# Two residual tiles for each stream, the next input asked for at the head of a turn, and the table request of the second experts moved into their inner loop

## The chip, the cores and the metric

The kernel runs on one NeuronCore of one Trainium2 chip, in one launch. The metric is the device time of the launch in microseconds (us); of several runs the median is given. TensorE does matmuls, VectorE and ScalarE element-wise work, GpSimd the small powers, memsets and indexed transfers, and SyncE (SP) starts transfers (DMA) between HBM and the on-chip memory. In the profile these engines are PE (PEld for its weight loads), DVE, ACT, POOL and SP. Each engine runs its own list of instructions in order; they meet in semaphores.

## What is computed

A decoder of four layers over 32 sequences of 128 tokens with 128 features. Each layer has three sections, and each section adds its result to the residual x after a layer norm:

```python
x = x + L0_attn(layernorm(x))           # delta rule with convolutions and a gate over four paths
x = x + L0_xattn(layernorm(x), ctx)     # 16 heads
x = x + L0_ffn(layernorm(x))
x = x + L1_attn(layernorm(x))           # 16 heads, causal
x = x + L1_xattn(layernorm(x), ctx)     # a mix with the mean of the context
x = x + L1_ffn(layernorm(x))            # 8 experts, 2 chosen, and a shared one
x = x + L2_attn(layernorm(x))           # 16 heads, causal, rotary
x = x + L2_xattn(layernorm(x), ctx, mask)
x = x + L2_ffn(layernorm(x))            # 14 experts, 1 chosen, GELU
x = x + L3_attn(layernorm(x))           # state-space scan
x = x + L3_xattn(layernorm(x), ctx, key_padding)
x = x + L3_ffn(layernorm(x))            # 8 experts, 1 chosen, limited capacity
```

The "second experts" are L2_ffn: for each of 14 experts `gelu(x @ w1 + b1) @ w2 + b2`, weighted and summed. L3_ffn depends on the order of all tokens, so the main loop only scatters each token's row to its expert's place in HBM, and a final stage computes those experts.

## The kernel before

**Streams and rounds.** Two streams work at once on every engine, each on a group of 2 sequences (256 tokens): stream 0 begins a round with L0_delta, stream 1 with L1_mix (ROUND, TURN and FIRST near the top of the file). A round has all twelve sections for both. Stream 0 therefore hands over from one group to the next at the end of a round, stream 1 in the middle of it, between L3_moe and L0_delta. There are 8 groups for each stream. They are run as a first stretch (stream 1 alone, L0_delta to L1_attn), a loop with a body of two rounds that runs three times, and a last stretch of one round and one part named "last". In the body the rounds are turn 0 and turn 1. A stretch and each pass of the loop body end with a barrier of all engines, before which SP waits until the awaited inputs have landed (`landed`, lines 2510 to 2513) and after which it clears the semaphores.

**The order.** Each section gives, for each engine, a Python generator, and the order of the two streams' steps on an engine is written out by hand as strings (TURNS and END_TURNS): "0" and "1" take the next step of that stream. On TensorE a "w" stands for one filler matmul of the identity (`warm`, line 2548), which keeps the engine active and whose result nobody reads. The order never depends on what is ready: an engine stands at its next instruction until its semaphores allow it. PSUM is a ring of 8 banks; an engine waits for a full bank with `P.take` and frees it with `P.give`.

**The residual.** Each stream has one tile `xres` of 128 x 2 x 128 floats. `norm_dve` (lines 694 to 708) reads it, `residual_dve` (line 714) and the second experts (line 1387) add to it, and in L3_moe line 1437 copies it into the rows to be scattered. SP's part of a handover is `stored` and `load`: it waits until the rows are made (`e3.placed`), starts the store of `xres` to the output (line 2455), waits for it and for the two indexed transfers of GpSimd (line 2459), and then starts four transfers, one for the next `xres` (line 2439) and three for the context, the mask and the key padding (lines 2440 to 2442). VectorE waits for the first of them (semaphore `s_in`) ahead of L0_delta's norm. That wait also keeps L0_delta from writing over the rows in the shared scratch before they have been scattered, since SP starts the input only behind them. SP's own order for two rounds is the string "011100011100".

At stream 1's handover, VectorE's order is: the norm of stream 0's cross attention (line 708 for 0_hn), the statistics of stream 1's new input (line 694), then for stream 0 the keys (line 996) and the masked keys (line 1006), whose first half TensorE's scores (line 864) wait for, then stream 1's normalized rows (line 708 for 1_hn) and the maxima of the scores (line 1013). GpSimd's part of L0_delta begins with one power for the norm and, when TensorE's transposes have been copied to hT, three memsets in the scratch (lines 2360 to 2362).

**Activation tables.** ScalarE can evaluate one set of functions at a time; a change of set is one instruction, ACT_TABLE_LOAD. `Tables.use` (line 429) asks for a set unless its record `now` says that it is in place. The record follows the order in which the steps of both streams are written out. In the second experts the request for the GELU set stands at the head of an expert, two steps of the order ahead of its first half:

```python
for e in range(E2):
    yield
    tables.use(act, GELU)
    for c in range(2):
        yield
        t = P.take(act, f"{nm}.u{e}.{c}")
```

Between these yields the other stream's attention may ask for the EXP set (line 977). Where an activation is reached with another set in place than it needs, the compiler puts a table load of its own ahead of it; the profile shows such a load with the line of the activation. For the first half of an expert from the fourth on, ScalarE waits for two banks (the one to read, and that of the expert three before, whose hidden rows it writes over); such a double wait is an instruction of its own.

## Time and profile before

| | us |
|---|---|
| median of 3 runs | 4257.61 |
| lowest and highest | 4251.89, 4261.13 |
| the profiled execution | 4248.77 |
| its span, first to last instruction | 4246.9 |
| TensorE busy | 3921.6 (92%) |
| VectorE busy | 3004.1 (71%) |
| ScalarE busy | 1983.9 (47%) |
| GpSimd busy | 655.7 (15%) |
| mean granted TensorE clock | 0.963 |

The busy times come from one execution recorded by the hardware profiler; the span is its own, and 1.9 us lie around it. A wait is written as "idle, <- who ended it"; "issue" stands where the profile names no releaser. Times "at" a point are microseconds from the start of the span. A row of the timeline can merge instructions of one kind that follow each other (x2, x8). The granted clock is a share of 2.4 GHz: 1.00 is 2.4, 0.50 is 1.2, and a value between is the mean over a stretch that has both.

### The profile page before, as it was taken

What the parts mean: (1) busy time and instruction counts of PE and PEld (TensorE: products, weight loads), DVE (VectorE), ACT (ScalarE), POOL (GpSimd) and SP (SyncE); (2) the same over time, 40 slices, a digit from 0 to 9 for tenths busy, and PEclk for the clock granted to TensorE, in tenths of its full rate; (3) what the DMA queues carried; (4) which work ended last, traced back from release to release, by engine and by line L of the source; (5) the groups of instructions that cost most, each with busy time, mean ns of one, the idle gap of its engine ahead of it and who ended that gap; (6) DMA issues with size and microseconds to landing.
All of it is one profiled execution on the core that took longest, in us unless ns stands there. A gap on an engine that the chain in (4) does not pass through costs nothing. (4 is left out here: it accounts for less than half of the span.)

```text
span 4246.9 us, 103906 instructions
## 1 busy us (share of the span) xinstructions
PE 3921.6 (92%) x42881; PEld 2849.9 (67%) x42881; DVE 3004.1 (71%) x7740; ACT 1983.9 (47%) x4472; POOL 655.7 (15%) x924
## 2 busy tenths in 40 slices
PE   4889999899998999989999899999999899999998
PEld 3667676667766676766866667666676667666685
DVE  5558786586865867768776787758786586876762
ACT  2355443655336453464534644365443655336441
POOL 2200212101120111201111020200212102120003
PEclk7899999999999989999999999999999999999999
DMA  3300000000000000000000000000000000000011
GB/s 92 76 2 1 10 1 10 1 3 8 9 2 1 9 2 9 2 1 9 2 9 2 1 9 2 9 2 1 10 1 10 1 1 9 8 2 1 3 37 66
DMA packets 52824, 46.08 MB, mean 11 GB/s; under 512 B 8354, under 2 KB 48914, under 8 KB 52126
## 3 DMA queue, kind: packets, MB, share of 16 engines
q1 hardware_dynamic: 48076, 32.94, 2.9%
q8 instruction: 346, 5.67, 0.6%
q0 software_dynamic: 2560, 5.79, 0.4%
q14 instruction: 128, 1.05, 0.1%
q10 hardware_dynamic: 1714, 0.63, 0.1%
HBM read 27.25 MB, written 12.62 MB: 9 GB/s over the span
## 5 line engine op out<-in xcount | busy, mean ns | idle before, releaser
L2548 PE MATMUL banks<-ident_bf 128*128 128x256 bf16 x6321 | 1004.5, 279 | 32.1 <-ACT scratch L979 11.5
L2548 PEld LDWEIGHTS banks<-ident_bf 128*128 128x128 bf16 x6321 | 619.0, 101 | 250.8 <-issue 78.7
L1013 DVE TENSOR_REDUCE scratch<-banks 128x4 f32<-128x512 f32 x512 | 321.8, 683 | 64.6 <-PE banks L837 29.7
L979 ACT ACTIVATE scratch<-banks 128x512 f32<-128x512 f32 x512 | 274.0, 598 | 148.8 <-PE banks L834 70.8
L1842 DVE TENSOR_TENSOR_SCAN scratch<-scratch 128x512 f32<-128x512 f32 x256 | 312.6, 1221 | 8.9 <-ACT scratch L1785 3.8
L1021 DVE RECIPROCAL scratch<-banks 128x128 f32<-128x128 f32 x128 | 122.4, 957 | 273.7 <-PE banks L919 247.3
L429 ACT ACT_TABLE_LOAD x242 | 310.5, 1283 | 6.3 <-PE banks L1189 2.0
L864 PE MATMUL banks<-scratch 32*128 32x512 f32 x2048 | 307.2, 654 | 4.7 <-issue 3.9
L1697 PE MATMUL banks<-scratch,w_ident 128*128 128x256 f32 x1024 | 268.3, 384 | 17.1 <-DVE scratch L1848 17.0
L685 POOL TENSOR_TENSOR 0_rstd<-0_var,minus_half 128x2 f32<-128x2 f32 x96 | 68.9, 718 | 1343.5 <-DVE 0_var L703 1030.9
L1785 ACT ACTIVATE scratch<-scratch,ssm_A 128x256 f32<-128x256 f32 x512 | 226.2, 500 | 98.0 <-DVE scratch L1842 91.3
L1362 ACT ACTIVATE scratch<-banks,w_e_b 128x256 f32<-128x256 f32 x448 | 195.0, 472 | 157.3 <-PE banks L1318 153.6
L919 PE MATMUL banks<-scratch 128*32 128x128 f32 x4096 | 216.7, 284 | 53.6 <-ACT scratch L979 52.2
L1326 PE MATMUL banks<-experts,scratch 128*128 128x128 f32 x1792 | 249.2, 286 | 6.5 <-DVE scratch L2249 5.9
L1983 PEld LDWEIGHTS banks<-scratch 32*32 32x32 f32 x10496 | 196.4, 114 | 86.9 <-issue 64.6
L1326 PEld LDWEIGHTS banks<-experts,scratch 128*128 128x128 f32 x1792 | 236.1, 199 | 26.0 <-issue 17.0
L1983 PE MATMUL banks<-scratch 32*32 32x32 f32 x10496 | 232.0, 201 | 15.3 <-issue 12.2
L685 POOL TENSOR_TENSOR 1_rstd<-1_var,minus_half 128x2 f32<-128x2 f32 x96 | 70.3, 732 | 939.5 <-DVE 1_var L703 671.5
L919 PE MATMUL banks<-scratch,w_slots 128*32 128x128 f32 x4096 | 209.9, 277 | 0.0
L1697 PEld LDWEIGHTS banks<-scratch,w_ident 128*128 128x128 f32 x1024 | 178.0, 190 | 47.4 <-DVE scratch L1848 23.8
L1238 ACT ACTIVATE scratch<-banks 128x256 f32<-128x256 f32 (+1 forms) x224 | 84.8, 383 | 251.8 <-PE banks L1189 251.3
L690 ACT COPY 0_hT<-banks 128x256 f32<-128x256 f32 x96 | 35.8, 373 | 349.2 <-PE banks L680 349.2
(515 smaller groups left out, 8041.5 us busy)
## 6 DMA issues: line engine op xcount, KB each, us to landing
expert_in<-scratch SPq DMA_DIRECT2D x1, 4112.0 KB, 27.0
experts<-in_e_W SPq DMA_DIRECT2D x14, 256.0 KB, 5.3
scratch<-expert_in SPq DMA_DIRECT2D x2, 1542.0 KB, 11.2
w_e_W<-in_e_W SPq DMA_DIRECT2D x3, 704.0 KB
experts<-in_e_w SPq DMA_DIRECT2D x1, 1792.0 KB, 8.2
experts<-in_e_w SPq DMA_DIRECT2D x2, 896.0 KB, 12.3
scratch<-expert_in SPq DMA_DIRECT2D x2, 514.0 KB, 4.4
1_xres<-in_x SPq DMA_DIRECT2D x8, 128.0 KB, 2.2
```

The source lines that it names most:

```text
L429: act.preload_act_table_set(name)
L864: last = pe.matmul(row_tiles(t), lhs[r, col(s)], rhs[r, s], start=True, stop=letter == "S" and mask is None, skip_group_check=True)
L919: last = pe.matmul(t[32 * i:32 * i + 32, k * L:(k + 1) * L], W["slots"][:, 32 * j:32 * j + 32] if k else vslot[:, s, j, i, :], pT[:, s % 2 ...
L979: P.give(act.activation(pT[:, s % 2, j, :], t, ACT.Exp), f"{nm}.T{s}{j}")
L1013: P.give(dve.tensor_reduce(negm[:, s, NI * j:NI * j + NI], row_tiles(t), X, ALU.max, negate=True), f"{nm}.S{s}{j}")
L1326: last = pe.matmul(t[:, col(s)], hid[:, e % RING, c, col(s)], w2[:, 2 * e + c, :], start=c == 0, stop=c == 1, skip_group_check=True)
L1362: P.give(act.activation(hid[:, e % RING, c, :], t, ACT.Gelu, bias=W["e2_b1"][:, 2 * e + c:2 * e + c + 1]), f"{nm}.u{e}.{c}")
L1697: last = pe.matmul(total[:, c * N:(c + 1) * N], ident[:], yc[:, k % RING, j, :], start=False, stop=n == DS - 2 and j == 1, skip_group_chec ...
L1785: ins = act.activation(decay[:, k % RING, j, :], dstart[:, c, :], ACT.Exp, scale=ssm_A[:, c, n + j:n + j + 1])
L1842: dve.tensor_tensor_scan(*flat, 0.0, ALU.mult, ALU.add).then_inc(ev(nm + ".state"), 1)
L1983: last = pe.matmul(t[dst, h * width:(h + 1) * width], lhs(h), rhs(h), start=True, stop=True, skip_group_check=True)
L2548: pe.matmul(banks[:, bank, 0:N].rearrange("p (s f) -> p s f", s=G), ident_bf[:], spread(ident_bf[:], G), start=True, stop=True, skip_group ...
```

## The change

It has two parts.

1. In the second experts, `tables.use(act, GELU)` moves from the head of an expert to the head of each of its two halves, behind the yield and ahead of the wait for the bank.
2. Each stream gets two residual tiles, `residual[0]` and `residual[1]`. `xres(name)` picks one by the turn and, for stream 1, by whether the section belongs to the group that the round began with or to the next. The input for the next group is started at the head of a turn (`load_x`), into the tile that is not in use; the context, the mask and the padding are started where they were (`load_ctx`). As VectorE's wait for the input no longer says anything of the scattered rows, SP adds 1 to a new semaphore, `s_taken`, when the store and the scatter are done, and GpSimd waits for it ahead of L0_delta's memsets. The new semaphore is cleared with the others.

```diff
--- before.py
+++ after.py
@@ -390,6 +390,7 @@
         self.ring.wait_given(eng, self.tag + name)
 
 
+KEYS = ["d0", "x0", "f0", "a1", "m1", "e1", "a2", "x2", "e2", "s3", "x3", "e3"]
 PER_PASS = {
     ".ctx.maskf": 1, ".ctx.ms": 1, ".ctx.n": 1, ".ctx.padrow": 1, ".ctx.rms": 1, ".ctx.sq": 1,
     "d0.Nb": 2 * G, "d0.T": 5 * G, "d0.TT": G, "d0.diag": 2 * G, "d0.feat": 1, "d0.inverse": 1, "d0.kb": 2, "d0.mid": 1,
@@ -627,7 +628,7 @@
 
         def stream(u):
             scratch = scratches[u]
-            xres = sb(f"{u}_xres", [128, G, D])
+            residual = [sb(f"{u}_xres{k}", [128, G, D]) for k in range(2)]
             ctx_tok = sb(f"{u}_ctx_tok", [128, G, D])
             ctxT = sb(f"{u}_ctxT", [128, N])
             ctxnT = sb(f"{u}_ctxnT", [128, N])
@@ -645,7 +646,7 @@
             var, rstd, rms, rms2 = (sb(f"{u}_{n}", [128, G]) for n in ("var", "rstd", "rms", "rms2"))
             place = sb(f"{u}_place", [128, G], U32)
             token = W["token"][:, TURN[u] * G:TURN[u] * G + G]
-            s_scatter = sem(f"rows_placed{u}")
+            s_scatter, s_taken = sem(f"rows_placed{u}"), sem(f"rows_taken{u}")
             s_in, s_out, s_ctx = sem(f"group{u}_loaded"), sem(f"group{u}_stored"), sem(f"context{u}_loaded")
             def program(ring, passes):
                 stacks, norms, shared = {}, {}, {}
@@ -655,8 +656,15 @@
                     P = PassBanks(ring, turn)
                     loads = 1 if part == "first" else turn + (ROUND[u][0] != "L0_delta")
 
+                    ended = 0 if part == "first" else loads
+                    lead = len(SECTIONS) - ROUND[u].index("L0_delta") if FIRST[u] and part == "round" else 0
+
                     def before(name):
                         return turn * PER_PASS[name[1:]]
+
+                    def xres(name):
+
+                        return residual[(turn + (KEYS.index(name[1:3]) < lead)) % 2]
 
                     ctx = f"{u}.ctx"
 
@@ -691,7 +699,7 @@
 
                     def norm_dve(dve, q, nm, rms_too=False):
                         for s in range(G):
-                            m = q.mark(dve.bn_stats(stats[:, s, :], xres[:, s, :]))
+                            m = q.mark(dve.bn_stats(stats[:, s, :], xres(nm)[:, s, :]))
                         first = m - G + 1
                         for s in range(G):
                             q.wait(first + s)
@@ -705,14 +713,14 @@
                         yield
                         dve.wait_ge(ev(f"{u}.rstd"), norm(nm) + 1)
                         for s in range(G):
-                            dve.tensor_scalar(hn[:, s, :], xres[:, s, :], mv[:, s, 0:1], rstd[:, s:s + 1],
+                            dve.tensor_scalar(hn[:, s, :], xres(nm)[:, s, :], mv[:, s, 0:1], rstd[:, s:s + 1],
                                               ALU.subtract, ALU.mult).then_inc(ev(f"{u}.hn"), 1)
 
                     def residual_dve(dve, q, name):
 
                         t = P.take(dve, name)
-                        P.give(dve.tensor_tensor(xres[:].rearrange("p s f -> p (s f)"), xres[:].rearrange("p s f -> p (s f)"), t,
-                                                 ALU.add), name)
+                        x = xres(name)[:].rearrange("p s f -> p (s f)")
+                        P.give(dve.tensor_tensor(x, x, t, ALU.add), name)
                         P.wait_given(dve, name)
 
                     def bias_row(pe, t, row, start=True):
@@ -1352,9 +1360,9 @@
                             act.activation(lg, tmp, ACT.Exp).then_inc(ev(f"{u}.exp"), 1)
                             for e in range(E2):
                                 yield
-                                tables.use(act, GELU)
                                 for c in range(2):
                                     yield
+                                    tables.use(act, GELU)
                                     t = P.take(act, f"{nm}.u{e}.{c}")
                                     if e >= RING and c == 0:
                                         P.take(act, f"{nm}.d{e - RING}")
@@ -1384,8 +1392,8 @@
                                 yield
                                 t = P.take(dve, f"{nm}.d{e}")
                                 for s in range(G):
-                                    ins = dve.scalar_tensor_tensor(out=xres[:, s, :], in0=t[:, col(s)],
-                                                                   scalar=gate[:, s, e:e + 1], in1=xres[:, s, :],
+                                    ins = dve.scalar_tensor_tensor(out=xres(nm)[:, s, :], in0=t[:, col(s)],
+                                                                   scalar=gate[:, s, e:e + 1], in1=xres(nm)[:, s, :],
                                                                    op0=ALU.mult, op1=ALU.add)
                                 P.give(ins, f"{nm}.d{e}")
                                 P.wait_given(dve, f"{nm}.d{e}")
@@ -1434,7 +1442,7 @@
                             tables.use(act, EXP)
                             act.wait_ge(ev(f"{u}.diff"), base["diff"] + 1)
                             act.activation(lg, tmp, ACT.Exp).then_inc(ev(f"{u}.exp"), 1)
-                            act.copy(rows[:, :, D:2 * D], xres[:]).then_inc(ev(nm + ".placed"), 1)
+                            act.copy(rows[:, :, D:2 * D], xres(nm)[:]).then_inc(ev(nm + ".placed"), 1)
 
                         def dve_f(dve, q):
                             yield from norm_dve(dve, q, nm)
@@ -2357,6 +2365,8 @@
                             norm_pool(pool, nm)
                             yield
                             P.wait_given(pool, nm + ".hT")
+                            if ended:
+                                pool.wait_ge(s_taken, ended)
                             pool.memset(pads[:, :, :, 0:3], 0.0)
                             pool.memset(TT64_flat, 0.0)
                             pool.memset(vpad[:, :, 0:PAD], 0.0).then_inc(ev(f"{u}.zero"), 1)
@@ -2435,11 +2445,17 @@
                     r_d = out.rearrange("(g u s) t f -> u g t s f", u=STREAMS, s=G)[at_v]
                     p_d = dram["key_pad"].rearrange("(g u a s) t -> u g a (s t)", u=STREAMS, a=1, s=G)[at_v]
 
-                    def load(sp, g):
-                        sp.dma_start(xres[:], x_d[g]).then_inc(s_in, 16)
+                    def load_x(sp, g, k):
+                        sp.dma_start(residual[k][:], x_d[g]).then_inc(s_in, 16)
+
+                    def load_ctx(sp, g):
                         sp.dma_start(ctx_tok[:], c_d[g]).then_inc(s_ctx, 16)
                         sp.dma_start(mask_i[:], m_d[g]).then_inc(s_ctx, 16)
                         sp.dma_start(pad_row_u8[:], p_d[g]).then_inc(s_ctx, 16)
+
+                    def load(sp, g):
+                        load_x(sp, g, 0)
+                        load_ctx(sp, g)
 
                     def stored(sp, g):
 
@@ -2452,14 +2468,17 @@
                             for e in range(E3 - 1):
                                 load_expert3(sp, e, s_e3)
                         sp.wait_ge(ev(f"{u}e3.placed"), G + 3 + before(f"{u}e3.placed"))
-                        sp.dma_start(r_d[g], xres[:]).then_inc(s_out, 16)
+                        sp.dma_start(r_d[g], residual[turn % 2][:]).then_inc(s_out, 16)
                         yield
                         sp.wait_ge(s_out, 16 * (turn + 1))
 
                         sp.wait_ge(s_scatter, g * (16 * G) + 16 * G)
+                        sp.sem_inc(s_taken, 1)
 
                     def steps(engine, *args):
 
+                        if engine == 4 and part == "round":
+                            load_x(args[0], args[1] + turn + 1, (turn + 1) % 2)
                         yield
                         for name in order:
                             if name == "L0_delta" and engine == 2 and loads:
@@ -2494,7 +2513,7 @@
                             if name == "L3_moe" and engine == 4:
                                 yield from stored(args[0], args[1] + turn)
                                 if part == "round":
-                                    load(args[0], args[1] + turn + 1)
+                                    load_ctx(args[0], args[1] + turn + 1)
                                 yield
 
                     context = {0: ctx_pe, 1: ctx_act, 2: ctx_dve, 3: ctx_pool}
@@ -2512,7 +2531,7 @@
                     sp.wait_ge(s_in, 16 * total)
                     sp.wait_ge(s_ctx, 48 * total)
 
-                return ones[0][0], landed, steps, [s_in, s_out, s_ctx]
+                return ones[0][0], landed, steps, [s_in, s_out, s_ctx, s_taken]
 
             return program
```

## Rows read from the trace of the kernel before

**Rows 1.** The page: busy time of TensorE, and the filler matmuls of line 2548.

```profile
PE 3921.6 (92%) x42881; PEld 2849.9 (67%) x42881; DVE 3004.1 (71%) x7740; ACT 1983.9 (47%) x4472; POOL 655.7 (15%) x924
...
L2548 PE MATMUL banks<-ident_bf 128*128 128x256 bf16 x6321 | 1004.5, 279 | 32.1 <-ACT scratch L979 11.5
```

**Rows 2.** Waits of TensorE, 153 to 4160 us: total us, times, longest us.

```profile
PE banks L919 <- ACT scratch L979: 51.6, 28, 3.1
...
PE banks L864 <- issue: 3.5, 7, 1.1
```

**Rows 3.** ScalarE's groups: count, busy us, mean ns, idle us before them.

```profile
L429 ACT ACT_TABLE_LOAD x242 | 310.5, 1283 | 6.3 <-PE banks L1189 2.0
...
L1362 ACT ACT_TABLE_LOAD x31 | 39.8, 1283 | 2.0 <-PE banks L1318 0.2
...
L979 ACT ACT_TABLE_LOAD x29 | 37.2, 1283 | 0.5
```

**Rows 4.** Timeline of ScalarE, 295 to 313 us: start, us, what ran, idle before.

```profile
301.23 1.28 ACT L1362 ACT_TABLE_LOAD   x1
...
310.35 1.28 ACT L1362 ACT_TABLE_LOAD   x1 [0.22 <-PE banks L1318]
```

**Rows 5.** Timeline of all engines, 450 to 465 us: a handover of stream 1.

```profile
455.43 0.60 DVE L708 TENSOR_SCALAR 0_hn<-0_xres,0_mv,0_rstd 128x128 f32<-128x128 f32 x2 [0.84 <-POOL 0_rstd L685]
...
456.54 0.40 SPq L2439 DMA_DIRECT2D 1_xres<-in_x  x1
...
457.42 0.59 PE L850 MATMUL banks<-0_ctxT,w_x_Wk 128*128 128x256 f32 x2
...
458.81 0.49 DVE L694 BATCH_NORM_STATS2 1_stats<-1_xres 128x6 f32<-128x128 f32 x2 [2.77 <-DMA 1_xres<-in_x]
...
459.62 0.48 DVE L996 TENSOR_SCALAR scratch<-banks,w_x_bk 128x256 f32<-128x256 f32 x1
...
460.13 1.29 DVE L1006 TENSOR_TENSOR scratch<-scratch,w_in_four 128x512 f32<-128x512 f32 x2
...
460.92 1.14 PE L864 MATMUL banks<-scratch 32*128 32x512 f32 x8 [1.10 <-issue]
...
462.43 2.48 DVE L1013 TENSOR_REDUCE scratch<-banks 128x4 f32<-128x512 f32 x4 [0.48 <-PE banks L837]
...
463.72 0.12 POOL L2360 MEMSET scratch<- 128x18 f32 x1 [2.31 <-ACT 1_hT L690]
```

**Rows 6.** Stream 1's residual tile, idle time before its instructions: us, times.

```profile
  DMA 1_xres<-in_x: 18.6, 8
```

**Rows 7.** Timeline of VectorE, 0 to 5 us.

```profile
3.46 0.48 DVE L694 BATCH_NORM_STATS2 1_stats<-1_xres 128x6 f32<-128x128 f32 x2 [3.46 <-DMA 1_xres<-in_x]
```

**Rows 8.** Timeline, 3506 to 3513 us: the last handover of stream 1.

```profile
3512.01 1.14 PE L864 MATMUL banks<-scratch 32*128 32x512 f32 x8 [0.18 <-issue]
```

**Rows 9.** Timeline, 644 to 664 us: a handover of stream 0.

```profile
654.39 0.38 SPq L2439 DMA_DIRECT2D 0_xres<-in_x  x1
...
660.38 0.48 DVE L694 BATCH_NORM_STATS2 0_stats<-0_xres 128x6 f32<-128x128 f32 x2
```

**Rows 10.** Waits of SP, 1150 to 1180 us, at the end of a loop body.

```profile
SPq L2574 <- PEq L2574: 1.8, 1, 1.8
```

**Rows 11.** SP's line 2459: duration ns min/median/max, first and last start.

```profile
L2459 SPq EVENT_SEMAPHORE  x8: 17/17/17, 654.2 to 3707.7; - x8
```

**Rows 12.** ScalarE's line 2089, its idle time: us, times.

```profile
  POOL scratch L2362: 0.8, 1
```

**Rows 13.** Rounds of stream 0 without a barrier: length, busy us (x), PEclk, DMA share, GB/s.

```profile
1174.83:1690.41 515.58, 487.19 (x5303) 353.53 (x5304) 372.32 (x963) 246.12 (x556) 77.88 (x110) 0.95 0.02 5
...
sum 2031.15, PE 1916.52 PEld 1391.26 DVE 1487.78 ACT 983.88 POOL 311.98; mean PE 479.13 PEld 347.82 DVE 371.94 ACT 245.97 POOL 78.00
```

**Rows 14.** Two stretches, same columns.

```profile
1025.00:1035.00 10.00, 9.89 (x125) 8.38 (x119) 4.02 (x15) 4.82 (x16) 0.71 (x1) 0.92 0.01 2
1035.00:1047.00 12.00, 12.00 (x46) 9.41 (x45) 6.97 (x20) 4.15 (x10) 0.11 (x1) 0.50 0.00 1
```

## The prediction, made before the changed kernel was run

> **What bounds the kernel now.** The page first. TensorE is busy 3921.6 of 4246.9 us, and 1004.5 us of that are 6321 filler matmuls of line 2548, which stand in its fixed order and compute nothing [rows 1]. So a shorter wait elsewhere can give back at most TensorE's own idle time, 4246.9 - 3921.6 = 325 us, and only where TensorE waits for exactly the thing that the change makes earlier. The second view is therefore TensorE's waits between 153 and 4160 us: the longest entry is 51.6 us in 28 waits for the exponentials of line 979; the waits at line 864, for which the profile names no releaser, are 3.5 us in 7 [rows 2]. Then I read ScalarE's groups for the first half of the change, and one handover of a stream for the second.
>
> **Part 1, the table loads.** Line 429, the explicit request, made 242 loads of 1283 ns. 31 more stand at line 1362 and 29 at line 979: there the record of the table in use was out of date, because the other stream had changed the table between two steps, and the load was put in by itself just ahead of the activation [rows 3]. After the change the record is right, so these 60 become explicit loads. ScalarE's order of work is the same, so their number is the same: each of the 60 really changes the set. I found no explicit load that went unused and would now be saved. What changes is only whether a load starts before or after the wait for the bank. The same rows price this: the 29 loads of line 979 sat idle 0.5 us in all, 17 ns each, so they already start without a wait; nothing is to be had there. The 31 of line 1362 sat idle 2.0 us. The floor is 31 x 17 ns = 0.5 us, so the wait that can be covered is 1.5 us. It lies at some loads only: the one at 310.35 began 0.22 us late, the one at 301.23 not at all [rows 4]. Bounds: a gain of 0 (if TensorE doesn't feel it) to 2.0 us. I take **-1.5 us**, since the exponentials behind such loads are what TensorE waits for [rows 2]. The 60 loads themselves, 60 x 1.283 = 77 us of ScalarE, stay.
>
> **Part 2, the input rows.** Stream 1 hands over in the middle of a round. SP waits for its result to be stored and its rows to be scattered, and issues the next input at 456.54. VectorE, done with stream 0's norm at 455.43 + 0.60 = 456.03, stands until 458.81, 2.77 us, for that input [rows 5]. Over the run this wait is 18.6 us in 8 [rows 6]; one of them, 3.46 us, is the very first load [rows 7] and stays. The seven others are 15.1 us. With two tiles the input is issued in the turn before, hundreds of microseconds ahead, so VectorE's 15.1 us go.
>
> What TensorE gets of it is less. Behind the norm VectorE makes the masked keys (lines 996 and 1006), for which TensorE's line 864 waits. TensorE was ready at 460.92 - 1.10 = 459.82. After the change line 996 starts when its bank is full, at 457.42 + 0.59 = 458.01, not at 459.62. The first half of line 1006 then ends 1.6 us earlier, at about 459.2 instead of 460.8, which is 0.6 us before TensorE needs it [rows 5]. So the whole 1.10 us goes here, and not more. In the last of the seven handovers TensorE's wait is only 0.18 us [rows 8]. All seven are the 3.5 us at line 864 [rows 2]. What is late next: VectorE's line 1013 already waits 0.48 us for TensorE's masks [rows 5], so from there TensorE leads and the other engines move with it. I take **-3.5 us**. Bounds: 0, if the shift is lost further on, and 15.1 us, if every microsecond of VectorE counts.
>
> Stream 0 hands over at the end of a round. Its input was issued at 654.39; with the 458.81 - 456.54 = 2.27 us that stream 1's took, it was there by 656.7, but VectorE comes to it at 660.38 without idle time [rows 9]. Gain 0; the cover is some 3.7 us of the other stream's work, which stays. The same holds where the loop body ends: the context loads still follow the store there and are awaited, and when all have landed SP waits a further 1.8 us for TensorE's queue [rows 10]. Leaving the input out lets the context loads go some 0.4 us earlier, into that 1.8 us. I take 0; were TensorE early by over 1.8 us, up to 0.4 us at each of three barriers would be felt.
>
> **What it adds.** The two input loads at the head of a turn cost SP 0.40 us each [rows 5]. Behind them in its queue is only the wait for stream 1's rows, half a round away. At the second turn stream 0's load stands behind its context loads and stream 1's behind that; each is needed only at that stream's next handover. GpSimd gets 11 waits on the new semaphore (7 of stream 1; of stream 0 only the 4 at second turns). Behind each in its queue are the three memsets of the delta section and then its later products, which ScalarE, VectorE and TensorE take up. The semaphore is raised where the input was issued before, at 456.5, while the memsets start at 463.72, released by the hT copy [rows 5]. If TensorE is 1.1 us early, they start at 462.6, still 6 us behind. A satisfied wait I price by SP's plain semaphore instruction, 17 ns [rows 11]: 11 x 17 = 0.2 us on GpSimd, bounds 0 and 0.2, taken as 0, because only one ScalarE copy of the run waited for those memsets, 0.8 us [rows 12].
>
> **Sum.** -1.5 - 3.5 = -5.0 us. The profiled execution took 4248.8 (span 4246.9), so one like it would take 4243.8. The median of the runs, 4257.6, lies 8.8 above it; the prediction is made for that: 4257.6 - 5.0 = **4252.6 us**, -0.12%. About 0.2%, 8.5 us, is what a measurement of this kernel can tell from no change, so this counts as no change.
>
> **Why runs differ.** The four rounds of stream 0 that hold no barrier have the same instructions. One of them took 515.58 us at 0.95 of TensorE's clock; the four together took 2031.15, so the others averaged 505.2 [rows 13]. The excess is 10.4 us, twice my sum. It isn't a matter of long waits: from 1035 to 1047 us TensorE was granted 0.50, 1.2 GHz, though it was busy 9.89 of the 10 us before and 12.00 of the 12 in it [rows 14]. The Trainium skill, "TensorE: Matmul & The Clock Gate", Part 1, has the throttled state as the default, which activity releases; by that rule shorter waits could only raise the clock, and the slower rival below would have no ground. By that rule a fall at a TensorE so busy should not be there, so it isn't relied on here: I leave the clock out of the sum and keep both signs.
>
> **Rivals.**
> - All of VectorE's wait arrives: 15.1 + 1.5 = 16.6 us, 4241.0. It would be so if VectorE set the pace behind the handover. Against it: the 0.48 us for which it waits on TensorE right there [rows 5]. For it: each set of four maxima behind it takes VectorE 2.48 us [rows 5]. Chance 0.12. The Trainium skill, "DMA: Bandwidth & Descriptors", in its rules table, would have the load's fixed cost overlap once it is issued early and waited for late; taken for the time of the kernel, that is this rival.
> - Nothing arrives: the 3.5 us turn up as another wait before the round ends, and the table loads were covered: 4257.6. Against it: TensorE releases every engine that feeds it there. Chance 0.12.
> - Slower, by the clock: the shift of a microsecond moves the dense stretches, and more rounds go as the long one did. It decides from two more: 2 x 10.4 - 5.0 = +15.8, 4273.4; one alone gives +5.4, 4263.0, still no change. Chance 0.08.
> - The same with the other sign: the long round becomes a short one, -10.4 - 5.0 = -15.4, 4242.2. Chance 0.10.
>
> **How the numbers follow.** My forecast has the remaining 0.58, with its own range 4248 to 4258 (the terms between 0 and what I took, and the runs' spread). The range 4242 to 4263 leaves out the first rival and the slower one, 0.20. Faster by over 0.2% is below 4249.1: 0.12 + 0.10, and 0.02 of the forecast, 0.24. Slower is above 4266.1: 0.07, as 0.01 of the slower rival stops at one round. Within: 0.69.
>
> **What would show it.** Right: no table load at lines 1362 and 979, about 302 at line 429, with about 1.5 us less idle before them all; VectorE's wait for the input left only at the start; TensorE's seven waits at line 864 gone; GpSimd's memsets still released by the hT copies. Wrong: another number of table loads; GpSimd waiting for SP; another TensorE wait near the handover grown by what line 864 lost; a round's length changed by more than 2 us at an equal clock.

## The result, and the profile after

| | before | after |
|---|---|---|
| median of 3 runs, us | 4257.61 | 4223.67 |
| lowest and highest, us | 4251.89, 4261.13 | 4217.96, 4225.45 |
| the profiled execution, us | 4248.77 | 4225.45 |
| its span, us | 4246.9 | 4223.6 |
| mean granted TensorE clock | 0.963 | 0.967 |

The ratio of the runs is 0.9934, with a 95% interval from 0.9912 to 0.9955: faster by 0.66%, 28 us by the ratio and 34 by the medians. The same kernel run again, six times against eleven of the kernel before, gave 0.993, 0.9913 to 0.9946. Forecast were 4252.6, in a range from 4242 to 4263. So the kernel gained some 23 to 29 us more than the 5.0 of the sum.

The page of the kernel after, to be held against [rows 1, 3]:

```profile
PE 3903.9 (92%) x42881; PEld 2838.5 (67%) x42881; DVE 3003.1 (71%) x7740; ACT 1980.7 (47%) x4470; POOL 655.9 (16%) x924
...
L2567 PE MATMUL banks<-ident_bf 128*128 128x256 bf16 x6321 | 995.5, 277 | 32.9 <-ACT scratch L987 10.8
...
L430 ACT ACT_TABLE_LOAD x300 | 384.9, 1283 | 7.3 <-PE banks L1197 2.0
```

TensorE has the same 42881 matmuls and is busy 3921.6 - 3903.9 = 17.7 us less; its 6321 fillers take 9.0 us less (277 ns each, not 279). The same work taking less time is the first sign that the clock had a part. All table loads are now at the explicit request, 300, and none is left at the two activations; their idle time is 7.3 us where the three rows of before had 6.3 + 2.0 + 0.5 = 8.8.

TensorE's waits, 153 to 4160 us, against [rows 2] (total us, times, longest):

```profile
PE banks L927 <- ACT scratch L987: 51.1, 29, 3.1
...
PE banks L872 <- ACT scratch L957: 0.8, 1, 0.8
```

The seven waits at the masks' line, 3.5 us, are gone; the one left there, 0.8 us, is ScalarE's. The handover of stream 1, timeline of all engines, against [rows 5]:

```profile
459.90 0.60 DVE L716 TENSOR_SCALAR 0_hn<-0_xres,0_mv,0_rstd 128x128 f32<-128x128 f32 x2 [0.84 <-POOL 0_rstd L693]
...
460.42 0.48 DVE L702 BATCH_NORM_STATS2 1_stats<-1_xres 128x6 f32<-128x128 f32 x2
...
461.88 0.59 PE L858 MATMUL banks<-0_ctxT,w_x_Wk 128*128 128x256 f32 x2
...
462.51 0.48 DVE L1004 TENSOR_SCALAR scratch<-banks,w_x_bk 128x256 f32<-128x256 f32 x1 [1.20 <-PE banks L858]
...
463.03 1.29 DVE L1014 TENSOR_TENSOR scratch<-scratch,w_in_four 128x512 f32<-128x512 f32 x2
...
464.22 1.14 PE L872 MATMUL banks<-scratch 32*128 32x512 f32 x8
```

VectorE goes from stream 0's norm (459.90) to stream 1's (460.42) without the 2.77 us for the input. Its masked keys (line 1004) wait only for their bank, full at 461.88 + 0.59, and TensorE's masks (line 872) start at 464.22 with no gap. The wait for stream 1's input has gone from 18.6 us in 8 to 3.4 us in 1, the very first. GpSimd's memset behind the new semaphore is still released by the hT copy:

```profile
467.01 0.12 POOL L2370 MEMSET scratch<- 128x18 f32 x1 [4.01 <-ACT 1_hT L698]
```

A round of stream 0 without a barrier, the one that took 515.58 us at 0.95 before [rows 13], and the sum of three such rounds of after (length, busy us of PE, PEld, DVE, ACT and POOL, PEclk, DMA share, GB/s):

```profile
1165.52:1669.51 503.99, 477.68 (x5303) 346.74 (x5304) 371.92 (x963) 245.78 (x556) 77.84 (x110) 0.97 0.02 5
...
sum 1507.69, PE 1424.07 PEld 1033.76 DVE 1114.77 ACT 737.38 POOL 233.63; mean PE 474.69 PEld 344.58 DVE 371.59 ACT 245.79 POOL 77.88
```

That round is 11.6 us shorter. With the first such round, 502.87 us, the four take 2010.6 us, 20.6 less than before, where the direct gain of a handover and the table loads is under 1 us a round on average (the 5.0 of the sum over seven rounds).

**Where the clock differs.** Before, in the second round, four stretches of TensorE's work at stream 1's gate, 60 to 105 us behind stream 1's handover, same columns:

```profile
1022.00:1032.00 10.00, 9.89 (x142) 8.62 (x140) 4.14 (x16) 6.80 (x23) 0.00 (x0) 1.00 0.01 2
1032.00:1047.00 15.00, 15.00 (x72) 11.68 (x70) 8.13 (x25) 4.78 (x12) 0.82 (x2) 0.54 0.00 1
1047.00:1057.00 10.00, 9.73 (x54) 5.97 (x54) 3.17 (x7) 8.10 (x17) 0.00 (x0) 1.00 0.00 0
1057.00:1064.00 7.00, 7.00 (x36) 5.30 (x36) 4.17 (x13) 6.31 (x10) 0.37 (x1) 0.51 0.01 2
```

After, four stretches that cover the same work (it comes 1.1 us earlier ahead of the falls and 7 us earlier behind them):

```profile
1015.00:1025.00 10.00, 10.00 (x253) 8.32 (x252) 4.50 (x16) 6.56 (x21) 0.00 (x0) 1.00 0.02 4
1025.00:1035.00 10.00, 9.89 (x125) 8.49 (x124) 4.31 (x16) 4.47 (x15) 0.82 (x2) 1.00 0.01 2
1035.00:1045.00 10.00, 10.00 (x63) 7.20 (x62) 8.35 (x25) 6.93 (x17) 0.00 (x0) 1.00 0.01 2
1045.00:1055.00 10.00, 9.72 (x58) 6.86 (x58) 3.55 (x9) 9.52 (x15) 0.00 (x0) 0.83 0.01 2
```

TensorE is busy 9.7 of 10 us or more in every one of these. Before, the clock falls to 1.2 GHz at 1033 us for 13.7 us and at 1057 for 6.8. After, only a short fall remains. In the two timelines the same instructions stand side by side (start, us, what ran). Before:

```profile
1030.12 0.71 PE L1343 MATMUL banks<-w_e_b,scratch 14*128 14x128 f32 x4
...
1034.54 1.06 PE L1983 MATMUL banks<-scratch 64*64 64x32 f32 x8
1035.53 2.93 PE L1666 MATMUL banks<-0_hT,w_s_in 128*128 128x256 f32 x6
...
1038.46 1.75 PE L1983 MATMUL banks<-scratch 128*128 128x32 f32 x8
...
1068.96 0.60 PE L1693 MATMUL banks<-scratch,skip_diag 128*128 128x256 f32 x2
```

After:

```profile
1029.54 0.71 PE L1351 MATMUL banks<-w_e_b,scratch 14*128 14x128 f32 x4
...
1033.45 0.65 PE L1991 MATMUL banks<-scratch 64*64 64x32 f32 x8
1034.03 1.56 PE L1674 MATMUL banks<-0_hT,w_s_in 128*128 128x256 f32 x6
...
1035.54 0.98 PE L1991 MATMUL banks<-scratch 128*128 128x32 f32 x8
...
1060.30 0.60 PE L1701 MATMUL banks<-scratch,skip_diag 128*128 128x256 f32 x2
```

Six matmuls of line 1666 take 2.93 us at half clock, and as line 1674 1.56 at full clock, in the same order behind the same gate matmuls (line 1983, now 1991). The order of the work is the same; what differs is only when it comes. The same stretch in all seven rounds, 30 us ahead of the first matmul of line 2065 of stream 1's gate to 16 us behind, below called **the spot**, in the kernel before:

```profile
518.00:564.00 46.00, 45.61 (x437) 36.69 (x436) 28.51 (x77) 29.27 (x69) 3.77 (x4) 0.96 0.01 1
1026.00:1072.00 46.00, 45.62 (x309) 35.13 (x308) 24.88 (x64) 24.76 (x54) 3.77 (x4) 0.78 0.00 1
1546.00:1592.00 46.00, 45.90 (x292) 35.26 (x291) 24.51 (x62) 23.36 (x49) 3.77 (x4) 0.74 0.00 1
2050.00:2096.00 46.00, 45.62 (x435) 36.61 (x436) 28.39 (x75) 29.32 (x70) 3.78 (x4) 0.96 0.01 1
2556.00:2602.00 46.00, 45.90 (x416) 36.35 (x415) 26.32 (x71) 29.27 (x69) 3.77 (x4) 0.89 0.01 1
3061.00:3107.00 46.00, 45.90 (x416) 36.42 (x415) 26.35 (x70) 29.25 (x69) 3.77 (x4) 0.89 0.01 1
3570.00:3616.00 46.00, 45.90 (x416) 36.48 (x405) 26.73 (x70) 28.88 (x68) 3.77 (x4) 0.89 0.01 1
```

and in three of the seven of the kernel after:

```profile
521.00:567.00 46.00, 45.61 (x440) 36.59 (x435) 28.34 (x75) 29.38 (x70) 3.77 (x4) 0.96 0.01 1
1019.00:1065.00 46.00, 45.61 (x479) 36.56 (x465) 28.05 (x73) 29.74 (x71) 3.77 (x4) 0.96 0.01 1
...
2538.00:2584.00 46.00, 44.59 (x494) 36.05 (x481) 27.94 (x73) 29.84 (x72) 3.77 (x4) 1.00 0.01 1
```

A stretch of 46 us at a mean clock c loses at most (1 - c) x 46 us, since TensorE is busy in nearly all of it. Before that makes 0.89 x 46 = 41 us over the seven (0.04 + 0.22 + 0.26 + 0.04 + 3 x 0.11), after 0.24 x 46 = 11 (six times 0.04, once 0), 30 us less. It is an upper bound: not every instruction takes twice as long at half clock (the six matmuls above 2.93 us against 1.56, the eight of 64 rows 1.06 against 0.65). The instructions themselves give the loss more exactly. From the four matmuls of line 1343 to the first of line 1693 behind the spot's fillers TensorE has the same work in every round of both kernels. In the round shown this takes 1068.96 - 1030.12 = 38.84 us before and 1060.30 - 1029.54 = 30.76 after, and 29.1 in after's fifth round, which has no fall in it, as in every such round of the kernels below with the same work there. The seven rounds take 240.8 us before and 213.7 after, where seven of 29.1 would be 203.7: **37 us lost before, 10 after, 27 us gained at the spot**.

Counted over 160 to 4150 us, the clock records of the two traces hold 218 us at half clock before and 188 after. At the spot they are 61 us fewer, so elsewhere they are some 31 more, which gives back at most 15 us of the 27. The spans differ by 23.3 us. What the spot and the places elsewhere leave of that, some 11, stands for the direct gain and whatever else differs between two executions.

### The profile page after: what moved, and what is told of

Read it like the earlier page. It is cut to its first block and busy times, and to the rows that moved or that the text cites. A ratio compares the mean times of both kernels' runs of the same rounds, so it can differ in the third digit from the quotient of the medians.

```text
span 4223.6 us, 103921 instructions
## 1 busy us (share of the span) xinstructions
PE 3903.9 (92%) x42881; PEld 2838.5 (67%) x42881; DVE 3003.1 (71%) x7740; ACT 1980.7 (47%) x4470; POOL 655.9 (16%) x924
```

## The experiments

Seventeen kernels and a repeat of the kernel after. The ratio is to the kernel before on the same chip, with its 95% interval; "range" is the highest run less the lowest; "lost at the spot" is the bound (1 - c) x 46, summed over the seven stretches. It comes from the one execution that was profiled, which can be one of the slowest (late_input, after_near16, before_less8) or of the fastest (after_near8) of its kernel.

| kernel | median | ratio | range | lost at the spot |
|---|---|---|---|---|
| before (all chips, medians and runs) | 4236 to 4261 | 1 | 4225 to 4274 | 41 |
| after | 4223.7 | 0.9934 [0.9912, 0.9955] | 7 | 11 |
| after_again | 4220.2 | 0.9930 [0.9913, 0.9946] | 8 | 14 |
| table_only | 4245.4 | 0.9977 [0.9959, 0.9994] | 19 | 40 |
| x_only | 4222.6 | 0.9926 [0.9902, 0.9950] | 6 | 12 |
| before_shift | 4250.3 | 0.9999 [0.9978, 1.0020] | 30 | 54 |
| after_shift | 4221.1 | 0.9920 [0.9896, 0.9945] | 11 | 16 |
| late_input | 4261.4 | 1.0002 [0.9983, 1.0020] | 39 | 54 |
| before_p10 | 4252.3 | 0.9999 [0.9980, 1.0018] | 30 | 39 |
| before_m10 | 4246.5 | 0.9970 [0.9952, 0.9989] | 30 | 46 |
| after_p10 | 4228.4 | 0.9931 [0.9907, 0.9954] | 20 | 17 |
| after_m10 | 4214.8 | 0.9917 [0.9899, 0.9934] | 13 | 7 |
| before_near16 | 4250.9 | 1.0031 [1.0010, 1.0053] | 36 | 27 |
| after_near16 | 4259.3 | 1.0042 [1.0023, 1.0061] | 37 | 65 |
| after_near8 | 4227.0 | 0.9971 [0.9955, 0.9987] | 27 | 4 |
| before_less8 | 4225.6 | 0.9959 [0.9941, 0.9977] | 32 | 46 |
| before_moved10 | 4216.7 | 0.9920 [0.9901, 0.9938] | 6 | 0 |
| after_moved10 | 4215.4 | 0.9919 [0.9900, 0.9937] | 16 | 3 |
| before_spot10 | 4222.1 | 0.9942 [0.9921, 0.9964] | 5 | 0 |
| after_moved_m20 | 4211.8 | 0.9917 [0.9894, 0.9939] | 11 | 0 |

The change repeated without an edit:

> The changed kernel once more, beside the next three on the same chip. Any theory: a ratio of 0.990 to 0.995 to the kernel before, 28 us.

**Each half alone, and a shift of everything.** table_only and x_only are the change's two parts; the shift adds 16 fillers once, at the end of the first stretch, to the kernel before and to the one after.

```
table_only (before)                      x_only (after)
 for e in range(E2):                      for e in range(E2):
     yield                                    yield
-    tables.use(act, GELU)               +    tables.use(act, GELU)
     for c in range(2):                       for c in range(2):
         yield                                    yield
+        tables.use(act, GELU)           -        tables.use(act, GELU)

before_shift, after_shift, behind the first stretch's turns on TensorE
+    if first:
+        for _ in range(16):
+            warm(pe, P)
```

> Part 1 alone: the table request inside the loop over halves, one residual tile. Theory A: direct gain 1.5 us (60 loads move from lines 1362 and 979 to the request's line); the rest by the clock, anywhere between 4225 and 4262. Rival B: 4256, no gain. Rival C (ScalarE's loads ahead of the bank are worth most of it): 4226 to 4232, with the exponentials' waits of TensorE, 51.6 us in 28, shorter by 20 us or more.

> Part 2 alone: two residual tiles and the early input, the table request left where it was. Theory A (the clock's falls moved by a small shift do most of it): the direct gain is the 4.0 us that the seven handovers gave back at full clock in the changed kernel; the rest of the 34 us of the medians comes or goes with the falls of the granted clock, so this version may stand anywhere between 4215 and 4255, and its time minus 4.0 follows the microseconds that it spent at half clock. Rival B (the early input itself is worth the 34 us): 4224 to 4228, with TensorE's position in the order of work ahead by over 4 us at every handover, at an equal clock. Rival C (the table request does it): 4253, no better than 4250.

> The kernel before, with 16 more filler matmuls on TensorE at the end of the first stretch, ahead of its barrier: nothing in the loop changes, all of it starts about 1.3 us later. Theory A: the falls of the clock come at other points of the same work, and the time moves by more than the 1.3 us added, up to some 25 us either way. Rivals B and C: 4257.6 + 1.3 = 4259, within the runs' spread of 5.

> The changed kernel with the same 16 filler matmuls at the end of the first stretch. Theory A: as for the kernel before, the time moves by more than the added 1.3 us if the changed kernel owes its time to where its clock falls; up to 4250. Rivals B and C: 4223.7 + 1.3 = 4225.

The early input alone brings the whole gain, 0.9926. The table loads alone measure 0.9977. The 1.5 us of the sum would be 0.9996, just above the interval's end of 0.9994. But the falls at the spot are as before (40 us), x_only has the whole gain without this part, and late_input below has this part and gains nothing. So no gain by the clock is shown for it. The page of x_only shows again the same matmuls in less time, 3921.6 - 3892.8 = 28.8 us of TensorE:

```profile
PE 3892.8 (92%) x42881; PEld 2831.4 (67%) x42881; DVE 3002.5 (71%) x7740; ACT 1982.0 (47%) x4472; POOL 655.4 (16%) x924
```

The one-time shift changes neither kernel. So it isn't that the change moved the whole program against the clock once; what matters recurs in every round.

**Two tiles, input issued late.** The changed kernel with both residual tiles and the new semaphore, the input of the next group issued at the old place.

```
 def steps(engine, *args):
-    if engine == 4 and part == "round":
-        load_x(args[0], args[1] + turn + 1, (turn + 1) % 2)
     ...
+    load_x(args[0], args[1] + turn + 1, (turn + 1) % 2)
     load_ctx(...)
```

> The changed kernel, but the next input is issued where it was before, behind the store (it still goes to the other tile). VectorE's wait for it at stream 1's handover comes back, 2 us in each of seven, and with it TensorE's wait at line 864, 0.2 to 1.1 us in each. Direct loss at an equal clock 3.5 to 4 us. Theory A1 (the length of the way from one place to another within a round decides how often the clock falls behind it; the early input made it shorter): about 4249, all of the gain gone, with more falls to half clock some 60 to 90 us behind the handover. Rival B1 (the second tile itself, its addresses, does it): 4222, the gain stays. Rival B2 (only the direct loss): 4226.

Everything is lost again: 1.0002. TensorE's wait at the masks is back, and so is VectorE's for the input:

```profile
PE banks L872 <- issue: 8.3, 7, 2.3
```

```profile
  DMA 1_xres<-in_x: 23.4, 8
```

8.3 us in 7 is more than twice before's 3.5, and 23.4 in 8 compares with 18.6 [rows 2, 6]; why they are longer is not shown. Two of its seven stretches at the spot, same columns as above:

```profile
1034.00:1080.00 46.00, 45.62 (x310) 35.11 (x309) 24.87 (x63) 24.82 (x55) 3.77 (x4) 0.78 0.01 1
...
2069.00:2115.00 46.00, 45.90 (x290) 35.26 (x289) 24.16 (x61) 23.73 (x50) 3.77 (x4) 0.74 0.00 1
```

So the second tile, the addressing and the semaphore do nothing that shows. The early issue does it, by 4 to 8 us of TensorE's waiting directly and by the falls that come or go with it. The stretch from line 1343's matmuls to line 1693's, 240.8 us over seven rounds before, takes 254.2 here and 214.8 in x_only.

**Work added or taken away behind the spot's first falls.** TensorE's written order has a run of 47 fillers near the spot's end (at 1063.6 us in the second round of before). It became 57 or 37 in every round.

```
(shortened; the same in END_TURNS[0])
-TURNS[0]: ... "w" * 47 ...
+TURNS[0]: ... "w" * 57 ...      (p10)     "w" * 37 ...      (m10)
```

> The kernel before with 10 filler matmuls more in each round (57). Rival B2: 4249 + 7.7 = 4257. Theory A1: off that line by more than 5 us, either way.

> The kernel before with 10 filler matmuls fewer in each round (37 in the run of 47). Direct gain at most 7.7 us, 4241.5, and less if VectorE isn't ready for the shorter run. Theory A1: the rounds get as short as the changed kernel's, and the time moves by more than that, for instance to 4225; or, if the place within the round matters and not its length, by 7.7 or less. Rival B2: 4241.5 to 4249.

> The changed kernel with 10 more filler matmuls in each of the seven rounds, in the run of 47 (now 57) that stands some 90 us behind stream 1's handover; at 0.11 us each that is 1.1 us a round, 7.7 us in all. Theory A1: the time moves by clearly more or less than +7.7, for instance back to 4249, since every round is 1.1 us longer, as it was before the change. Rival B2: 4221 + 7.7 = 4229.

> The changed kernel with 10 fillers fewer in each round's run of 47. Direct: -7.7 us on the changed kernel (the kernel before gained 0.3% by it), ratio 0.990 to 0.992. If the 47 were needed to keep the clock up behind it: slower than the changed kernel.

Ten fillers here are 1.1 us a round, 7.7 us of the run, 0.0018 of the ratio. The kernel before didn't feel ten more (0.9999) and went 0.3% faster with ten fewer. The kernel after hardly felt ten more (0.9931 where it had 0.9934 and 0.9930) and went from 4220.2 to 4214.8 without ten, on the same chip. A change by 0.0018 from before or after lies within the interval of each of the four. None moved the falls by much: 39 and 46 us before, 17 and 7 after. Work behind the spot's first falls costs about itself.

**Work added between the handover and the spot.** Eight or sixteen fillers some 30 us behind stream 1's handover; and before_less8 takes eight away between 18 and 29 us behind it.

```
+TURNS[0] = TURNS[0][:958] + "w" * 16 + TURNS[0][958:]    (and "w" * 8; the same in the second round and in END_TURNS[0])

before_less8, in each round
+for at, n in (951, 2), (942, 3), (912, 3): take the n "w" at this place out
```

> The changed kernel with 8 more filler matmuls in each round, 0.9 us, about 30 us behind stream 1's handover and ahead of the place, some 70 us behind it, where the clock fell in the kernel before. Theory A2 (what counts is how far that place lies, in time, behind the fall that every round has in the other stream's attention some 150 us ahead of the handover; the early input shortened that way by 0.2 to 1.1 us): the way is as long as before the change, and the long falls come back, 4221 + 6 direct + 20 or so = 4240 to 4252. Rival (the early input helps by something else than this length): 4221 + 6 = 4227.

> The changed kernel with 16 fillers a round, 1.8 us, at the same place; 12 us in all. Theory A2: the way is now longer than it was before the change, past the lengths at which the long falls were seen, so it may cost no more than the 12 us, 4233, and be faster than with 8. Rival: 4233, but slower than with 8 by 6.

> The kernel before with 16 fillers more a round at that place, 12 us of work that nobody needs. Theory A2: the way is moved past the lengths of the long falls, and the kernel gets faster for it, 4249 + 12 - 27 = 4234 or so. Rival: 4249 + 12 = 4261, slower by 0.3%.

> The kernel before with 8 fillers fewer a round between 18 and 29 us behind the handover, 0.9 us or less, 6 us in all. Theory A2: the way gets as short as the early input made it, and the long falls go: 4249 - 6 - 20 = 4223 to 4230, most of the change's gain without the change. Rival: 4243 to 4249.

This is the sharpest result. Sixteen fillers, 16 x 0.11 = 1.8 us a round (27 together take 3.11 us there, in a row of before_near16's timeline), some 13 us of the run, turned 0.9934 into 1.0042: 46 us. (The kernel after itself wasn't run on this chip, so the two ratios are of two chips.) Two of the seven stretches and the sum of all seven, in after_near16:

```profile
521.00:567.00 46.00, 45.90 (x290) 35.28 (x289) 24.16 (x61) 23.72 (x50) 3.77 (x4) 0.74 0.00 1
...
3589.00:3635.00 46.00, 44.61 (x324) 35.07 (x324) 25.86 (x65) 24.89 (x55) 3.76 (x4) 0.85 0.00 1
sum 322.00, PE 317.85 PEld 246.92 DVE 177.93 ACT 169.18 POOL 26.36; mean PE 45.41 PEld 35.27 DVE 25.42 ACT 24.17 POOL 3.77
```

The falls are back in all seven, 65 us lost, where the profile of before has 41. The same fillers in the kernel before cost 1.0031, 13 us, their own work and no more. So a shift of 1.8 us ahead of the spot, in a kernel that keeps its early input, brings the falls back: it isn't TensorE's wait at the handover as such that makes them. after_near16 was forecast at 4233 and measured 4259.3, so the theory that it would be past the bad lengths failed, and the kernel before with the sixteen stood where its rival had it. The two runs with eight came out, by their ratios, near or between their two forecasts. after_near8's ratio is 0.4% above after's (0.9971 against 0.9934), some 16 us for 6 us of work, though its profiled execution (4212.5, the fastest of its twelve) shows hardly a fall. before_less8's ratio is 0.9959, 17 us (11 by the medians) for 6 us of work, though its profile (4241.2, its slowest) shows 46 us lost. One profile is one execution out of a wide range, and for these two it says little of the median. Both moved by more than their own work, in the direction that was forecast, and that the falls did it is not shown.

**Thicker work at the spot itself.** Ten fillers a round were put among the gate's small matmuls (3, 3, 2 and 2), and ten taken from the run of 47: the number of instructions is the same.

```
(shortened; in both rounds of TURNS[0] and in END_TURNS[0])
+for at, n in ((1152, -10), (1066, 2), (1065, 2), (1064, 3), (1063, 3)):
+    if n < 0: TURNS[0] = TURNS[0][:at] + TURNS[0][at - n:]
+    else:     TURNS[0] = TURNS[0][:at] + "w" * n + TURNS[0][at:]
```

> The kernel before with as many fillers as it had: in each round 10 of the run of 47 are taken away, and 10 are put among the small matmuls of stream 1's gate (line 1983, operands 64 rows high), just ahead of the point where the clock falls some 70 us behind the handover. Theory A3 (the clock falls there because TensorE does thin work then, and whether it does hangs on where the clock's judgement meets that work): with that work thickened the falls at that point go whatever their place, 78 to 109 us at half clock there become 30 or less, and the time goes down by 25 to 35 us, ratio 0.992 to 0.994, with no change to the handover. Rival (only lengths of ways matter, not what TensorE does there): no systematic gain but the direct one of a shorter run, ratio 0.997 as with 10 fewer alone.

> The same move of 10 fillers in the changed kernel. Theory A3: its falls at that point are few already (20 to 34 us at half clock), so it gains at most 10 us on the changed kernel, and stands no more than 5 us from the kernel before with the same move, less the direct 4 us of the early input. Rival: ratio 0.989 to 0.991, 27 us ahead of the kernel before with the same move.

Without anything of the change, the kernel before is at 4216.7, a little faster than the kernel after, and its five runs lie within 6 us where eleven of the kernel before lie within 21 on the same chip. With the change as well it is 4215.4: the two kernels, 31 us apart on this chip without these fillers (4251.5 and 4220.2), are 1.3 us apart with them. The rival with only the lengths of ways, 0.997, is excluded for the kernel before (0.9920, at most 0.9938).

**Only added, nothing taken away; and the version with the least work.**

```
before_spot10 (before):      (1066, 2), (1065, 2), (1064, 3), (1063, 3)
after_moved_m20 (after):     (1152, -20), (1066, 2), (1065, 2), (1064, 3), (1063, 3)
```

> The kernel before with ten filler matmuls a round added among the small gate matmuls of stream 1 and nothing taken away. Theory A3 (thin work of TensorE at this spot lets the granted clock fall, and fillers there hold it up): it does more work than the kernel before, at most 10 x 8 rounds of some 0.1 us = 8 us, and is still faster, because the falls at the spot, 82 us at half clock in the profile of before and so 41 us of time, are gone: 4257.6 - 41 + 8 = about 4225, ratio 0.990 to 0.995, and the windows of the spot show the full clock. Rival B3 (the gain of the kernel with moved fillers came from where the fillers were taken away): the falls stay or move by chance and the ratio is 1.000 to 1.004.

> The changed kernel with the ten fillers at stream 1's gate and the run of 47 further on cut to 27. Theory A3: no falls at the spot (at most 15 us at half clock there), and against the changed kernel with ten fillers moved (47 cut to 37), 0.9919, another ten fillers of some 0.1 us in each of eight rounds are gone: 4215 - 8 = about 4207 and a ratio of 0.989 to 0.991. Rival B4 (the fillers cover a wait for VectorE or hold the clock where they stand): what TensorE waits for takes their place, or falls come where they stood, and the ratio is 0.991 or above.

before_spot10 does all that the kernel before does and 70 fillers more, and is faster, 0.9942. Its page:

```profile
PE 3889.5 (92%) x42951; PEld 2826.9 (67%) x42951; DVE 3002.4 (71%) x7740; ACT 1982.0 (47%) x4472; POOL 655.0 (16%) x924
...
L2556 PE MATMUL banks<-ident_bf 128*128 128x256 bf16 x6391 | 994.2, 274 | 34.2 <-ACT scratch L987 11.5
```

Its 6391 fillers take 994.2 us, 10.3 less than the 6321 of before [rows 1], and TensorE's whole work 32.1 less. The fillers in TensorE's timeline, between the gate's matmuls of 64 rows:

```profile
1030.60 0.71 PE L1351 MATMUL banks<-w_e_b,scratch 14*128 14x128 f32 x4
1031.24 0.50 PE L2556 MATMUL banks<-ident_bf 128*128 128x256 bf16 x3
1031.67 0.66 PE L1991 MATMUL banks<-scratch 64*64 64x32 f32 x16
1032.26 0.50 PE L2556 MATMUL banks<-ident_bf 128*128 128x256 bf16 x3
1032.69 0.65 PE L1991 MATMUL banks<-scratch 64*64 64x32 f32 x8
```

and two stretches at the spot and the sum, at full clock in all seven:

```profile
1022.00:1068.00 46.00, 44.72 (x405) 35.61 (x399) 27.79 (x73) 28.55 (x67) 3.77 (x4) 1.00 0.00 1
...
3551.00:3597.00 46.00, 44.72 (x395) 35.64 (x396) 27.78 (x75) 28.26 (x66) 3.77 (x4) 1.00 0.01 1
sum 322.00, PE 313.02 PEld 249.39 DVE 193.97 ACT 200.33 POOL 26.36; mean PE 44.72 PEld 35.63 DVE 27.71 ACT 28.62 POOL 3.77
```

That settles it: the gain comes with the fillers at the spot and not from where fillers were taken away. The stretch from line 1343's matmuls to line 1693's takes 30.64 us in every round, 1.5 more than the 29.1 without these ten fillers, so they cost 1.5 us here and not the 1.1 that ten cost in the run of 47. The seven together take 214.5 us, 26.3 less than before, and the spans of the two profiles differ by 26.5. The six runs lie within 4.8 us; the kernel before's eleven, on the same chip and in between, within 31.7, from 4226.0 to 4257.7. The granted clock of that fastest execution was 0.966 and of that slowest 0.957. So the kernel before sometimes meets its clock well, and then costs little more than this one. after_moved_m20 is the fastest median of all, 4211.8, 0.3% under the kernel after's. It missed the 4207 that was expected, and its ratio, 0.9917, is above 0.991, as the rival wanted. But the kernel before ran faster in that comparison (4246.9 against 4251.5), its stretches at the spot are all at 1.00, and its span, 4207.6, is 7.4 us below that of after_moved10, which is the price of ten fillers a round; so I read it by the theory, and leave what the ratio says open within its interval. Against before_spot10, on the same chip, it is 10.3 us faster. It is the version to keep.

## Why the prediction was wrong

**Right: the direct terms.** Part 1 as forecast: no load at the two activations, with 1.5 us less idle before them. Their number is 300 and not 302; "another number of table loads" was named as a sign of being wrong, and by it the claim that each of the 60 really changes the set was off by two. Part 2 as forecast: the 15.1 us of VectorE gone, the seven waits of TensorE gone, the memsets still released by the hT copy, the masks' line without a gap. At each of the seven handovers the start of TensorE's masks (line 864, now 872), counted from TensorE's work ahead of the handover, came earlier by 1.17, 0.33, 0.89, 0.41, 0.52, 0.38 and 0.26 us: 4.0 where 3.5 were forecast. That the masks' bound was min(what VectorE gains, what TensorE waits) was the right way to read [rows 5]. With falls gone from the spot in both, the two kernels' medians differ by 1.3 us (after_moved10, before_moved10), which agrees with anything from 0 to some 7, as their runs range over 16 and 6 us: so the 5.0 is shown at the instructions and not resolved in the time.

**The rival "all of VectorE's wait arrives"** (4241.0) fell at its mechanism: of VectorE's 15.1 us only 4.0 reached TensorE. The Trainium skill, "DMA: Bandwidth & Descriptors", in its rules table, has the load's fixed cost overlap once it is issued early, and the trace agrees: VectorE's wait fell from 18.6 us to 3.4. Taken for the kernel's time that would have been 15.1 us, and the instructions show 4.0.

**Wrong: "I leave the clock out of the sum and keep both signs."** This is the step that failed. It took the falls of the clock for a scatter that a shift of a microsecond would throw either way, and gave as its largest cases one round shorter (-10.4) or two rounds longer (+20.8). What the runs showed: falls come at one place in all seven rounds, and lose 37 us there in the kernel before (41 by the bound). The early input takes 27 of these away (by the bound 11, 14 and 12 are left in after, its repeat and x_only), and the late input brings them back (54).

The rows for it were at hand. The long round [rows 13] holds the stretch of the spot at 0.74, and the stretch at 0.50 [rows 14] lies in the spot of the round before it. The prediction read the second as the reason for the first, though 1035 to 1047 us is outside the long round, which began at 1174.83: two rounds had the same fall at the same work, and this went unseen. The same stretch of all seven would have shown 0.78, 0.74 and three of 0.89, up to 41 us in reach. With those rows the clock is the largest term in play, some eight times the sum, and the range had to reach down to 4257.6 - 5.0 - 41 = 4212.

**Also wrong: "a round's length" as a coin toss.** The rival with the other sign had the right mechanism, the long round gets short, at -15.4 and a chance of 0.10; it was mis-sized, since it took one round of seven. Its mirror, "more long rounds", happened too, in after_near16: 46 us for some 13 us of work. Both signs are real; no rule found here says which one comes.

**The rule that was weighed.** TensorE was busy 15.00 of 15 us in the stretch at 0.54. The Trainium skill, "TensorE: Matmul & The Clock Gate", Part 1, has a clock that activity releases; read as busy time, it disagrees with this row. Fillers of 128 rows put between matmuls of 64 rows, with the engine busy before and after, took the falls away (44.72 of 46 us busy and 1.00, against 45.62 and 0.78). So a TensorE that is busy throughout is not for that alone granted its full clock. What it is in the fillers that does it, rows, columns or type, wasn't tried. Nor was a delay of the same length at the spot without matmuls; more work ahead of the spot (before_near16) or behind its first falls (before_p10) left falls of 27 and 39 us in the kernel before, where the fillers at the spot left none in three kernels and 3 us in a fourth. Small matmuls alone don't bring a fall either: in after_near8's profile five of the seven stretches are at 1.00 with no filler added at the spot.

**What stays open.** Why the early input makes the gate's work meet the clock well in nearly every round, and 1.8 us ahead of it undoes this in all seven, is not settled: the traces show that the moment matters and not by what rule. Nor is why there were some 31 us more at half clock elsewhere in the profile of after; the profiles with the ten fillers at the spot have as much elsewhere as before has (126 to 136 us against 136).

## What to carry to other kernels

List the granted clock of the same stretch of work in every round before costing an edit. If it falls where TensorE is busy with small matmuls, that term can be many times the microseconds that the edit moves, with either sign. Here the kernel whose own runs ranged over some 30 us was the one with such falls. Then try to mend the clock first, with a few full-height matmuls among the small ones: here ten a round gave 0.6% (0.9942) without any other change, brought the range of runs from 32 us to 5, and left an edit's direct worth to be measured.

## What the runs showed of the hardware that was not expected

- At the spot TensorE's mean granted clock is 0.54 over 15 us in which it is busy 15.00, in and just behind gate matmuls of 32 and 64 rows and 32 columns; with ten 128x256 matmuls among these it is granted 1.00 in all seven rounds.
- The same 29.1 us of TensorE's work take 38.84 us with 20.5 us of half clock in them and 39.95 with 23.9: a microsecond at half clock costs 0.45 to 0.48 here, not 0.5.
- A 128x256 bf16 filler added to a program can pay for itself: 70 more of them, and TensorE busy 3889.5 us where it was 3921.6.
- The runs of a kernel spread with its falls: over 5 to 20 us in those that lose up to 17 us at the spot (but for after_near8, 27), over 19 to 39 in those that lose 27 or more. The former have mostly 3 to 6 runs and the latter 12 and more, which alone widens a range; the 4.8 us in 6 against 31.7 in 11 on one chip is more than that.
